# Non-local attention on one core: the first image's q and k projected in full fp32, and one low part of x moved to GpSimd

## The reference

```python
B, Cc, W, H = x.shape                       # (4, 256, 32, 32)
xf = x.reshape(B, Cc, N)                    # N = W * H = 1024
q = jnp.einsum('oc,bcn->bon', Wq, xf) + bq[None, :, None]     # Wq: (32, 256)
k = jnp.einsum('oc,bcn->bon', Wk, xf) + bk[None, :, None]
v = jnp.einsum('oc,bcn->bon', Wv, xf) + bv[None, :, None]     # Wv: (256, 256)
scores = jnp.einsum('bqi,bqj->bij', q, k)
attn = jax.nn.softmax(scores, axis=-1)
out = jnp.einsum('bcj,bij->bci', v, attn)
return out.reshape(B, Cc, W, H) + x
```

## Time and profile before

| | before |
|---|---|
| median of 3 runs | 163.83 us (163.79 to 164.0) |
| the profiled execution's own time | 163.81 us |
| its span in the profile | 162.0 us, 2456 instructions |
| TensorE matmul busy | 157.5 us (97%), 788 matmuls |
| VectorE busy | 133.9 us (83%) |
| ScalarE busy | 109.2 us (67%) |
| GpSimd busy | 60.0 us (37%) |
| chain that ended last | TensorE 90%, DMA 2%, ScalarE 2%, VectorE 2% |

### The profile page before, as it was taken

How to read it: one execution, slowest core, us unless ns; L and a number is a source line. 1 busy time by engine, 2 the same in 40 slices (tenths; PEclk the granted TensorE clock), 3 DMA queues, 4 the chain that set the end, 5 groups by cost and what they waited for, 6 DMA issues and landing times.

```text
span 162.0 us, 2456 instructions
## 1 busy us (share of the span) xinstructions
PE 157.5 (97%) x788; PEld 132.3 (82%) x788; DVE 133.9 (83%) x215; ACT 109.2 (67%) x200; POOL 60.0 (37%) x68
## 2 busy tenths in 40 slices
PE   7999999999999999999999999999999999999993
PEld 5677887798888887798888897788888898888882
DVE  1899998888988989997989989895989779846952
ACT  3679887969999545827999646736896655756400
POOL 4479946256222316348443300342333300124500
PEclk9999999999999999999999999999999999999999
DMA  4576672152103030162711130162320330003003
GB/s 161 187 299 166 243 235 89 31 151 63 55 0 97 1 129 2 37 144 67 268 39 49 54 129 0 37 146 67 121 61 1 97 129 0 0 5 129 0 0 130
DMA packets 7780, 14.67 MB, mean 91 GB/s; under 512 B 1504, under 2 KB 2072, under 8 KB 7768
## 3 DMA queue, kind: packets, MB, share of 16 engines
q1 hardware_dynamic: 6728, 13.46, 25.4%
q0 software_dynamic: 608, 0.80, 2.2%
q10 hardware_dynamic: 432, 0.26, 0.5%
HBM read 4.79 MB, written 4.20 MB: 55 GB/s over the span
## 4 chain that ended last, share of the span: by engine, by line
PE 90%; DMA 2%; ACT 2%; DVE 2%; issue 1%; DVEq 0%
PE acc L1009 32%; PE acc L1015 16%; PE slot L849 11%; PE st L996 9%; PE slot L909 7%; PE slot L1009 5%; DMA small_sb<-small 2%; PE slot L1015 2%; ACT dump L504 2%; PE slot L861 2%; PE slot L866 2%; PE slot L935 1%; DVE negmax L667 1%; PE slot L881 1%; DVE x_lo L632 0%
## 5 line engine op out<-in xcount | busy, mean ns | idle before, releaser
L402 POOL TENSOR_TENSOR w_lo<-w_full,w_hi 128x512 fp32r<-128x512 f32 x21 | 28.0, 1338 | 46.6 <-ACT w_full L542 25.4
L1009 PE MATMUL acc<-w_hi,v_hi 128*128 128x512 f32 x112 | 44.3, 395 | 0.0
L1009 PE MATMUL acc<-w_hi,v_lo 128*128 128x512 f32 x112 | 44.1, 394 | 0.0
L542 ACT ACTIVATE w_full<-st 128x512 f32<-128x512 f32 x62 | 36.8, 594 | 7.6 <-PE st L996 7.5
L504 ACT ACTIVATE dump<-slot,negmax 128x1024 f32<-128x1024 f32 x29 | 32.5, 1119 | 10.5 <-DVE negmax L667 10.1
L667 DVE TENSOR_REDUCE negmax<-slot 128x1 f32<-128x1024 f32 x29 | 35.2, 1217 | 2.7 <-PE slot L909 2.7
L1015 PE MATMUL acc<-w_lo,v_hi 128*128 128x512 f32 x112 | 37.4, 396 | 0.0
L734 DVE TENSOR_TENSOR w_lo<-w_full,w_hi 128x512 fp32r<-128x512 f32 x43 | 30.7, 719 | 3.6 <-issue 0.5
L1009 PEld LDWEIGHTS acc<-w_hi,v_hi 128*128 128x128 f32 x112 | 21.1, 189 | 5.0 <-issue 0.2
L1009 PEld LDWEIGHTS acc<-w_hi,v_lo 128*128 128x128 f32 x112 | 21.2, 189 | 4.8
L1015 PEld LDWEIGHTS acc<-w_lo,v_hi 128*128 128x128 f32 x112 | 21.0, 188 | 4.8
(11 more groups left out here) (102 smaller groups left out, 225.2 us busy)
## 6 DMA issues: line engine op xcount, KB each, us to landing
out<-x_sb SPq DMA_DIRECT2D x7, 512.0 KB, 2.8
x_sb<-x SPq DMA_DIRECT2D x3, 1024.0 KB, 5.1
k_b<-k_a SPq DMA_DIRECT2D x8, 192.0 KB, 2.6
q_b<-q_a SPq DMA_DIRECT2D x8, 192.0 KB, 2.6
x_sb<-x SPq DMA_DIRECT2D x2, 512.0 KB, 4.2
k_a<-qk_parts SPq DMA_DIRECT2D x12, 64.0 KB, 2.0
q_a<-qk_parts SPq DMA_DIRECT2D x12, 64.0 KB, 2.2
k_a<-qk_parts POOLq DMA_DIRECT2D x6, 64.0 KB, 2.2
```

The lines of the kernel that those rows point to most:

```text
L402: nc.gpsimd.tensor_tensor(w_lo[:, r, :], w_full[:, r, :], w_hi[:, r, :].bitcast(fp32), ALU.subtract).then_inc(w_split_pool, 1)
L542: nc.scalar.activation(w_full[:, r, :], st_home(n), ACT.Exp).then_inc(exp_done, 1)
L1009: nc.tensor.matmul(dst, v[:, b % 2, j, c * P:(c + 1) * P], w_hi[:, n % RING, part], start=(j == 0 and v is v_hi), stop=False)
```

## The change

The first image's q and k projection becomes one plain fp32 matmul for each piece, straight from the loaded weights and the loaded x. For that the weights are loaded already doubled (each of k and q stands twice), so `small_sb` grows from 132 to 260 columns; `wqk_hi` and `wqk_lo` go, and with them VectorE's two operations. GpSimd now makes `wqk_pair` itself from the loaded weights (one cut, one subtraction). The matmuls on zeros go from 20 to 16. VectorE makes three of the four low parts of the first image's x; GpSimd makes the fourth (piece 3), between `put_q_dup(0)` and `put_q_dup(1)`, with a semaphore of its own. TensorE waits for the low parts only where v needs them. GpSimd's wait for the shifts moves ahead of the first `split_x1`, and its `split_w(1)` moves ahead of the third `split_x1`.

```diff
-        wqk_hi = sb("wqk_hi", [P, CT, P], fp32r)
-        wqk_lo = sb("wqk_lo", [P, CT, P], fp32r)
+        small_sb = sb("small_sb", [P, CT * P + 2 + CT])
...
 # GpSimd
-            for half, (parts, made) in enumerate(((wqk_hi, wqk_cut), (wqk_lo, wqk_split))):
-                pool.wait_ge(made, 1)
-                nc.gpsimd.tensor_copy(
...
+            pool.wait_ge(small_in, DMA)
+            nc.gpsimd.tensor_copy(pair(HI), wqk).then_inc(pair_made, 1)
+            pool.wait_ge(pair_made, 1)
+            nc.gpsimd.tensor_tensor(pair(LO), wqk, pair(HI).bitcast(fp32), ALU.subtract).then_inc(pair_made, 1)
             pool.wait_ge(pair_made, 2)
...
             put_q_dup(0)
             pool.wait_ge(q_dup_put, 1)
+
+            c, part = piece(3)
+            pool.wait_ge(x0_cut, 4)
+            nc.gpsimd.tensor_tensor(x_lo[:, 0, c, part], x_sb[:, 0, c, part],
+                                    x_hi[:, 0, c, part].bitcast(fp32), ALU.subtract).then_inc(x0_split_pool, 1)
+            pool.wait_ge(x0_split_pool, 1)
             put_q_dup(1)
             pool.wait_ge(q_dup_put, 2)
             split_q2()
             pool.wait_ge(q2_lo_put, 1)
             cut_x1(0)
+
+            pool.wait_ge(shift_ready, 1)
             split_x1(0)
             pool.wait_ge(x1_split, 1)
             cut_x1(1)
             split_x1(1)
             pool.wait_ge(x1_split, 2)
-
-            pool.wait_ge(shift_ready, 1)
             cut_x1(2)
+
+            pool.wait_ge(w_split_dve, SPLIT_COUNT[0])
+            split_w(1)
             split_x1(2)
             pool.wait_ge(x1_split, 3)
             cut_x1(3)
             pool.wait_ge(x1_cut, 4)
-
-            split_w(1)
             pool.wait_ge(w_split_dve, SPLIT_COUNT[2])
             split_w(3)
...
 # VectorE
-            nc.vector.tensor_copy(twice(wqk_hi), wqk).then_inc(wqk_cut, 1)
-            dve.wait_ge(wqk_cut, 1)
-            nc.vector.tensor_tensor(twice(wqk_lo), wqk, twice(wqk_hi).bitcast(fp32),
-                                    ALU.subtract).then_inc(wqk_split, 1)
-            for i in range(4):
+            for i in range(3):
...
 # TensorE
             def first_project_qk(i):
                 c, part = piece(i)
-                dst = qk_home(0, i % 2)
-                if i == 0:
-                    pe.wait_ge(wqk_cut, 1)
-                pe.wait_ge(x0_cut, i + 1)
-                nc.tensor.matmul(dst, wqk_hi[:, c, :], x_hi[:, 0, c, part], start=(c == 0), stop=False)
-                if i == 0:
-                    pe.wait_ge(wqk_split, 1)
-                nc.tensor.matmul(dst, wqk_lo[:, c, :], x_hi[:, 0, c, part], start=False, stop=False)
-                pe.wait_ge(x0_split, i + 1)
-                last = nc.tensor.matmul(dst, wqk_hi[:, c, :], x_lo[:, 0, c, part], start=False, stop=(c == CT - 1))
+                pe.wait_ge(x0_in[c], DMA)
+                last = nc.tensor.matmul(qk_home(0, i % 2), small_sb[:, c * P:(c + 1) * P], x_sb[:, 0, c, part],
+                                        start=(c == 0), stop=(c == CT - 1))
...
-            keep_busy(20, QUARTER)
+            keep_busy(16, QUARTER)
+            pe.wait_ge(small_in, DMA)
             for i in range(4):
                 first_project_qk(i)
             pe.wait_ge(wv_cut, 1)
+            pe.wait_ge(x0_split, 3)
             v_tile(0, 0)
             v_tile(0, 1)
...
             pe.wait_ge(rowsum_ready, 2)
+            pe.wait_ge(x0_split_pool, 1)
             v_tile(0, 4)
             v_tile(0, 5)
```

More of the change, by code:

```diff
@@ L69, in nonlocal_attention @@
         x_lo = sb("x_lo", [P, 2, CT, N], fp32r)
-        small_sb = sb("small_sb", [P, CT * 2 * CQK + 2 + CT])
-        bias = small_sb[:, CT * 2 * CQK:CT * 2 * CQK + 2]
-        bv_sb = small_sb[:, CT * 2 * CQK + 2:CT * 2 * CQK + 2 + CT]
-        wqk_hi = sb("wqk_hi", [P, CT, P], fp32r)
-        wqk_lo = sb("wqk_lo", [P, CT, P], fp32r)
+        small_sb = sb("small_sb", [P, CT * P + 2 + CT])
+        bias = small_sb[:, CT * P:CT * P + 2]
+        bv_sb = small_sb[:, CT * P + 2:CT * P + 2 + CT]
         wqk_pair = sb("wqk_pair", [P, CT, P], fp32r)
@@ L120, in nonlocal_attention @@
         ones_put = sem("ones_put")
-        wqk_cut = sem("wqk_cut")
-        wqk_split = sem("wqk_split")
         pair_made = sem("pair_made")
@@ L127, in nonlocal_attention @@
         x0_split = sem("x0_split")
+        x0_split_pool = sem("x0_split_pool")
         x1_cut = sem("x1_cut")
@@ L413, in split_x1, with pair @@
                                         x_hi[:, 1, :, quarter(i)].bitcast(fp32), ALU.subtract).then_inc(x1_split, 1)
-            for half, (parts, made) in enumerate(((wqk_hi, wqk_cut), (wqk_lo, wqk_split))):
-                pool.wait_ge(made, 1)
-                nc.gpsimd.tensor_copy(
-                    wqk_pair[:, :, half * 2 * CQK:(half + 1) * 2 * CQK].rearrange("p c (g r) -> p c g r", g=2),
-                    parts[:, :, :].bitcast(fp32).rearrange("p c (g d r) -> p c g d r", g=2, d=2)[:, :, :, 0, :],
-                ).then_inc(pair_made, 1)
+            wqk = small_sb[:, 0:CT * P].rearrange("p (c g d r) -> p c g d r", c=CT, g=2, d=2)[:, :, :, 0, :]
+            def pair(half):
+                return wqk_pair[:, :, half * 2 * CQK:(half + 1) * 2 * CQK].rearrange("p c (g r) -> p c g r", g=2)
+            pool.wait_ge(small_in, DMA)
+            nc.gpsimd.tensor_copy(pair(HI), wqk).then_inc(pair_made, 1)
+            pool.wait_ge(pair_made, 1)
+            nc.gpsimd.tensor_tensor(pair(LO), wqk, pair(HI).bitcast(fp32), ALU.subtract).then_inc(pair_made, 1)
             pool.wait_ge(pair_made, 2)
@@ L516, in add_bias @@
             def add_bias(c):
-                act.wait_ge(x0_split, 4)
+                act.wait_ge(x0_split, 3)
+                act.wait_ge(x0_split_pool, 1)
                 nc.scalar.activation(x_sb[:, 0, c, cols(0)], x_sb[:, 0, c, cols(0)],
@@ L1152 @@
         "small": np.ascontiguousarray(np.concatenate([
-            by_partition(np.concatenate([wk, wq], axis=0)),
+            by_partition(np.concatenate([wk, wk, wq, wq], axis=0)),
             np.stack([np.concatenate([bk, bk, bq, bq]), np.concatenate([bk, bq, bk, bq])], axis=1),
```

## The result

The changed kernel takes 164.78 us (median of 18 runs, 164.3 to 167.15) against 163.86 us (18 runs, 163.68 to 164.27) for the kernel before in the same rounds: ratio 1.0063, interval 1.0046 to 1.0081. It is slower by about 0.9 us, where no change was forecast. Four of its 18 executions took 166.6 us or more, the others 164.3 to 165.4; without those four the median is 164.63. The profiled execution took 164.97 us with a span of 163.2 us, so 1.16 us more than that of before.

A forecast was written before the change was run, and what follows sets the result against it. TensorE's own work was taken to bound everything after 18 us, so only the first row maximum's shift counted: -0.04 us from the projection, 0 from GpSimd's moved work, 163.81 to 163.77, about 163.8 (no change); range 163.3 to 164.8.

The forecast's parts named there:

- the first: After 18 us: TensorE is always busy, so the change acts only through when that stretch begins (17.69 us).
- Start of full fp32: First projection: the first full fp32 matmul starts at about 4.9 us, after the small weights land by 4.85.
- 0.92: First projection: us per full fp32 matmul at the higher clock, as four streams of 0.23; bounds 0.23 and 1.84.
- Rival 2: First projection: full fp32 costs more than four streams, for instance through unhidden weight loads; 164.4 to 164.9 us; chance 0.17.
- rival 3: First projection: full fp32 is cheaper, 0.23 us a matmul; at most -0.5 us, 163.3; chance 0.06.
- Clock: First projection: TensorE's clock rises at 5.4 us, so 0.25 us is lost to the lower level.
- rival 1: First projection: the clock rises at another moment; earlier 163.5 us (chance 0.15), later, at 6.5, 164.3 (chance 0.10).
- the 11.13 of the forecast: Front: the first row maximum on VectorE starts at about 11.13 us instead of 11.17, a shift of -0.04.
- Fourth low part on GpSimd: Between GpSimd's two copies of q: a subtraction of 1.29 us, cost 0, bounded by 0 and +0.2 us.
- The second image's x: On GpSimd: it waits for the shifts until 16.31 us; two low parts ready at about 19.7, needed at 27.64; cost 0.
- rival 4: At 23 us: GpSimd and VectorE get in each other's way; a whole operation costs 0.54 us, 164.3; chance 0.10.
- TensorE without idle time after 18 us: Sign to look for after 18 us: the forecast is wrong if TensorE waits at 24 us.

The follow-up runs named there:

- h1_after_1: The changed kernel with one memset more on VectorE, its column behind all other arrays: 164.02 us, ratio 1.001 to the kernel before.
- h4_before_pad: The kernel before the change with three one-column memsets more at the start of VectorE, nothing else: 164.8 us, ratio 1.0064.
- e5_order_alone: The kernel before with only GpSimd's new order (second image's x waits for the shifts, split of weight block 1 earlier): 163.97 us, ratio 1.0006.

## Why the prediction was wrong

The step that failed is the first: "nothing but TensorE's own work ... sets the time after 18 us, and the change can act only through the moment at which that stretch begins". TensorE was busy throughout, but with little to spare. In the trace of before the last transfer of q and k lands at 37.18, 0.05 us ahead of the matmul at 37.23, and GpSimd's weight split ends at 48.43 + 1.30 = 49.73, 0.77 ahead of the matmul at 50.50. The change takes instructions out of VectorE's stream (307 to 305), and its idle stretch moves from 101.75, where it did no harm, to 42 us. That was on no list of rivals. Shown: one needless instruction (h1_after_1) gives most of the loss back, and three (h4_before_pad) make a loss of the same size in the kernel before. The size: 0.76 us by the medians of 164.78 and 164.02 (0.6 from 164.63), where d grows by 0.5 at the matmul at 51 us and by 0.6 from 42 to 55 us.

The other points:

- Start of full fp32 "about 4.9": 4.90.
- "0.92" for a full fp32 matmul at the higher clock: 0.86, as two instructions 0.43 apart, with their loads of 0.19 hidden. Rival 2 (dearer) is refuted, rival 3 (0.23) too.
- Clock: taken at 5.4, it rose at about 6.6 in the profiled execution. That is rival 1's later rise, priced at +0.51 for 6.5; measured +0.48 at the first maximum. Over the thirteen profiles with full fp32 and a short gap the first maximum lies between 10.79 and 11.65, around the 11.13 of the forecast. So the sum of the front lies in the middle of what the profiles show, and its spread was too small. In the profiled execution two terms were off against each other: three full matmuls were 3 x 0.06 = 0.18 us cheaper, and the clock rose later. Without the loss behind 30 us the kernel stands at 164.02 with 16 matmuls on zeros (h1_after_1), 0.16 above before.
- The rule of the Trainium skill (TensorE: Matmul & The Clock Gate, What's actually happening) that the moment of the rise varies from start to start was cut to 0.2 us, by the three times of before. The profiles bear out more: 0.86 us between the earliest and the latest first maximum of those thirteen (kernels with 16 or 18 matmuls on zeros), and 11.79 in the one of h4_before_pad, whose front is that of before but for its memsets.
- Fourth low part on GpSimd, "cost 0": right. It ran from 9.71 to 11.00 between the copies of q.
- The second image's x, "cost 0", and rival 4 (GpSimd and VectorE at 23 us): VectorE's cut took 0.72 and its low part 0.91, but TensorE did not wait there. GpSimd's new order alone (e5_order_alone) measured 1.0006. The meeting that did cost was another one, at 44 us.
- "TensorE without idle time after 18 us" as the sign to look for: it did show the error, at 51 us.

The range, 163.3 to 164.8, holds 164.78 by its edge only, and that edge was rival 2's, which did not happen. That is luck.

## What to carry to other kernels

A bottleneck engine that never idles says nothing about slack: list the waits that end shortly ahead of it (0.05 and 0.77 us here), for every one of them can become the bound. An edit that adds or removes instructions on an engine can move such a stretch and such a packet, as it did on VectorE here; before a difference of half a per cent is put down to the edit, time the edit with one or two needless instructions more. When two kernels differ late, and the edit is early, look for rows whose idle time ends in "issue" and for packets on an instruction queue. The word alone is no sign (GpSimd's row at 48.43 before has it too); a stretch that moves with needless instructions is.

## What the runs showed of the hardware that was not expected

- Code arrives in packets on a queue that the profile calls "instruction", and where they fall can cost time. VectorE stood for 0.46 to 0.51 us at a place that moves with the length of its stream, with a packet of 8 KB 0.67 to 0.95 us behind, and a packet of 8 KB among transfers of 64 KB goes with about 0.4 us more for most of them and up to 0.9 for the last pair. The Trainium skill (Runtime: NRT & Kernel Launch, Instruction fetch mechanics) calls the crossing of a block "mostly hidden"; here the stretch at 42 us or the packet at 35 us cost 0.5 to 1.0 us of 164 (164.78 against 164.02, 164.28 against 163.65 and 163.82, 164.80 against 163.83), and the stretch at 102 us nothing that can be told. How one packet delays a transfer by that much, and why three memsets move the place so much farther than one or two, isn't shown.
- Of two subtractions on VectorE and GpSimd beside each other, the one that starts first ran at its own length: 0.12 or 0.28 us at their start decided which one lost 0.4 (GpSimd) or 0.9 us (VectorE).
- TensorE's clock fell back at 9.65 us, after two waits of 0.84 and 0.68 us, in the kernel whose projection was four single streams on zeros: with less to do, its first maximum came at 11.57, no earlier than before (11.17).
